# One more batch turned by VectorE, one list of requests for SyncE, and a new order at head and drain

## The chip, the cores and the metric

The kernel runs on one core of a Trainium2 chip, and the metric is the device time of that one core in microseconds. TensorE (PE) multiplies, VectorE (DVE), ScalarE (ACT) and GpSimd (POOL) do the elementwise work, and SyncE (SP) issues most of the DMA requests; ACT issues the others. The requests of SP go through DMA queue q1, those of ACT through q10, and both are served by the same 16 DMA engines.

## The reference

Two inputs `x` ("rgb") and `ctx` ("geo") of 16 batches, each 128 channels by 1024 positions in f32, attend to each other across channels, with 8 heads of 16 channels:

```python
rgb = jnp.transpose(rgb_emb, (0, 2, 1)); geo = jnp.transpose(geo_emb, (0, 2, 1))
def heads(x, w):
    return (x @ w.T).reshape(b, n, H, d).transpose(0, 2, 1, 3)
def xca(q, k, v):
    attn = softmax(einsum('bhni,bhnj->bhij', q, k) * scale, axis=-1)
    return einsum('bhnd,bhde->bhne', v, attn).transpose(0, 2, 1, 3).reshape(b, n, c)
res_p2r = xca(heads(rgb, wq_rgb), heads(geo, wk_point), heads(geo, wv_point)) @ proj_p2r.T
res_r2p = xca(heads(geo, wq_point), heads(rgb, wk_rgb), heads(rgb, wv_rgb)) @ proj_r2p.T
return transpose(rgb + res_p2r) + transpose(geo + res_r2p)
```

## The kernel before

Since the attention is over channels, everything that depends on positions enters through one 128x128 Gram matrix of a batch, `gt` times `xt`. For it both inputs must lie with the positions on the partitions ("turned"). A batch then goes through these products: turn (`turn_half`, only for some batches), Gram matrix (`gram_half`, two halves), `uv_product`, `s_product` (the scores), masking, exponents and `normalise` (the two softmaxes), `y_product`, `t_product` (a 256-column matrix, to which the identity is added for the residual), and the last product (`last_product`, two halves), which multiplies that matrix with `x` and `ctx` and yields the output. The last product is made of twelve 512-column matmuls, since each f32 operand is split in a high and a low fp32r part: ACT makes the high parts (`split_hi`, `t_high`), POOL the low parts of the inputs and DVE the other low parts.

The program is a pipeline written out by hand. In step i (the loop `for i in range(...)` that each engine has) batch i is turned, i-1 goes through the Gram matrix, i-2 through `uv` and `s`, i-3 through softmax, `y` and `t`, and i-4 through the last product. A step of PE begins with the last product of batch i-4. Each engine runs its list in the order written and waits at semaphores.

There are two ways of turning. Batches in `on_tensor` (0 to 4 and 9) are turned by PE with an identity matrix: eight groups of four matmuls into `xt_ps` and `gt_ps`, copied out by ACT (`copy_xt`) and DVE (`copy_gt`). Batches in `VECTOR_GROUPS`, five pairs, are loaded a second time with their 32x32 blocks already exchanged by the DMA (`load_turned`, into one of three slots of `xz` and `gz`) and DVE turns each block (L534). Such a pair is eight requests of 256 KB, four of SP and four of ACT. Groups 0, 1 and 2 are requested in steps 2, 4 and 6 (`first_steps`), groups 3 and 4 in the step after the last batch of the group whose slot they take has been turned.

Besides, every batch is loaded plainly (`load_plain`, two requests of 512 KB into one of six slots), and every output is stored by SP (`store`, 512 KB, from one of eight slots of `out_sb`). ACT's `evacuate(b, 0)` for b from 8 on waits until the store of batch b-8 has landed (L434). SP runs its requests step by step, L236 to L252; the stores come with a lag of seven steps.

Of the kernel before, what the change touches and what calls it, by code (L numbers as in the profile page):

```python
# [15 lines left out]
RAW_SLOTS = 6  # L16
SPLIT_SLOTS = 3
OUT_SLOTS = 8
STORE_LAG = 7
PAIRS = 3  # L20
OFF_HEAD = -3.0e38
WARM = 36
# [1 line left out]
WQR, WKR, WKP, WQP, PP, PR, WVP, WVR = range(8)  # L24


VECTOR_GROUPS = ((5, 6), (7, 8), (10, 11), (12, 13), (14, 15))


def bass_cross_channel_attention(nc: bass.Bass, x, ctx, weights, out):  # L30
# [20 lines left out]
    with ExitStack() as stack:  # L51
# [120 lines left out]
                eng.wait_ge(xt_copied, 2 * on_tensor.index(b) + 1 + half)  # L172


        first_steps = (2, 4, 6)
        issued_in = {first_steps[group] if group < PAIRS else VECTOR_GROUPS[group - PAIRS][-1] + 1: group
                     for group in range(len(VECTOR_GROUPS))}

# [35 lines left out]
        def _(sp):  # L214
            def load_plain(b):
                slot = b % RAW_SLOTS
                sp.dma_start(x_raw[:, slot, :], x[b]).then_inc(x_loaded[slot], 16)
                sp.dma_start(g_raw[:, slot, :], ctx[b]).then_inc(g_loaded[slot], 16)

            def store(b):  # L220
                sp.wait_ge(half_copied, 2 * b + 2)
                sp.dma_start(out[b], out_sb[:, b % OUT_SLOTS, :]).then_inc(out_stored[b % OUT_SLOTS], 16)
# [9 lines left out]

            for i in range(2, B):  # L236
                for b in range(5, B):
                    if i == max(2, b - 1 if b in on_vector else b - 3):
                        if b >= RAW_SLOTS:
                            sp.wait_ge(x_lo_ready, b - RAW_SLOTS + 1)  # L240
                            sp.wait_ge(g_lo_ready, b - RAW_SLOTS + 1)
                        load_plain(b)
                group = issued_in.get(i)
                if group is not None:
                    if group >= PAIRS:
                        pair_turned(sp, group - PAIRS)
                    load_turned(sp, x_turn, xz, xz_loaded, group, (0, 1))
                    load_turned(sp, g_turn, gz, gz_loaded, group, (0, 1))
                if i >= STORE_LAG:
                    store(i - STORE_LAG)  # L250
            for b in range(B - STORE_LAG, B - 1):
                store(b)  # L252
            last_slot = (B - 1) % OUT_SLOTS
            sp.wait_ge(half_copied, 2 * B - 1)
# [11 lines left out]
        def _(pe):  # L266
# [8 lines left out]
                                               ident2[:, 0, :])  # L275
                last.then_inc(done, 1)

            def turn_half(b, half):
                n = on_tensor.index(b)
                if n or half:  # L280

                    pe.wait_ge(xt_copied, 2 * n + half)
                turn(b, half, x_raw, x_first, x_loaded, xt_ps, xt_done)
                if n or half:
                    pe.wait_ge(gt_ready, 2 * b + 1 if half else 2 * on_tensor[n - 1] + 2)
                turn(b, half, g_raw, g_first, g_loaded, gt_ps, gt_done)

            def gram_half(b, half):
                x_turned_half(pe, b, half)
# [80 lines left out]
                nc.tensor.matmul(ps[:, P:2 * P], w_sb[:, WQP, :], uv[:, 1, :], start=True,  # L370
                                 stop=True).then_inc(s_done, 1)

            for i in range(B + 1):
                g, s, y, l = i - 1, i - 2, i - 3, i - 4
                if l >= 0:
                    last_product(l, 0)
                    if l != B - 4:
                        last_product(l, 1)
                    uv_product(s)
                if i in on_tensor:  # L380
                    turn_half(i, 0)
                if s >= 0 and l < 0:
                    uv_product(s)
                if y >= 0 and i not in on_tensor:
                    y_product(y)
                if g >= 0:
                    gram_half(g, 0)
                if y >= 0 and i in on_tensor:
                    y_product(y)
                if i in on_tensor:  # L390
                    turn_half(i, 1)
                if y >= 0:
                    t_product(y)
                if g >= 0:
                    gram_half(g, 1)
                if s >= 0:
                    s_product(s, s_ps)
# [8 lines left out]
            last_product(B - 3, 0, 3, 6)  # L406
            t_product(B - 2)
            last_product(B - 3, 1)
            y_product(B - 1)
            last_product(B - 2, 0, 0, 3)  # L410
            t_product(B - 1)
            last_product(B - 2, 0, 3, 6)
            last_product(B - 2, 1)
            last_product(B - 1, 0)
            pe.wait_ge(half_copied, 2 * B - 2)
# [5 lines left out]
        def _(act):  # L421
# [49 lines left out]
            for i in range(B + 1):  # L471
# [13 lines left out]
                    evacuate(l, 0)  # L485
                if l >= 0 and l != B - 4:
                    evacuate(l, 1)
                if group is not None:
                    load_turned(act, g_turn, gz, gz_loaded, group, (2,))
                if s >= 0:  # L490
                    copy_uv(s)
                if i in on_tensor:
                    copy_xt(i, 0)
                if group is not None:
                    load_turned(act, g_turn, gz, gz_loaded, group, (3,))
                if s >= 0:
                    split_hi(s, g_raw, g_loaded, g_hi, g_hi_ready)
                if i in on_tensor:
                    copy_xt(i, 1)
                if y >= 0:  # L500
                    t_high(y)
                if i == 1:
                    act.wait_ge(wu_loaded, 16)
                    nc.scalar.copy(wu_hi[:, :, :], w_sb[:, WQR:WKR + 1, :]).then_inc(wu_hi_ready, 1)
# [3 lines left out]
            copy_uv(B - 1)  # L508
            evacuate(B - 4, 1)
            split_hi(B - 1, x_raw, x_loaded, x_hi, x_hi_ready)  # L510
            evacuate(B - 3, 0)
            exponents(B - 1)
            t_high(B - 2)
            split_hi(B - 1, g_raw, g_loaded, g_hi, g_hi_ready)
            evacuate(B - 3, 1)
            evacuate(B - 2, 0)
            t_high(B - 1)
            evacuate(B - 2, 1)
# [136 lines left out]
```

## Time and profile before

| | |
|---|---|
| median of 3 runs | 127.03 us (125.57 to 127.28) |
| the profiled execution | 126.98 us, its span 124.9 us, 2.08 us lie around the span |
| PE busy | 117.1 us, 94% of the span |
| DVE, ACT, POOL busy | 59%, 67%, 62% |
| DMA | 36.35 MB, mean 291 GB/s; q1 73.9% and q10 17.7% of 16 engines' span |
| PE's granted clock | full in all 40 slices |

All times are microseconds from the start of the span. In the chain of waits a row gives the start, the length and what ran. In a timeline the engine, line, operation and shapes follow the start and the length; in brackets stands the idle time of the engine before the instruction and what ended it. "SPq" and "ACTq" are the DMA requests as the issuing sequencer runs them. "DMA to landing" is the time from the start of a request to the arrival of its last byte. PE's steps can be found in the chain by their last product (`out_ps L316 x12`).

### The profile page before, as it was taken

The numbers are of one execution on the slowest core, as the hardware profiler recorded it, in microseconds if no ns is written. First come the engines' busy times: TensorE is split into PE (matmuls) and PEld (weight loads), VectorE is DVE, ScalarE is ACT, GpSimd is POOL, SyncE is SP. The second block draws the span as 40 slices with busy tenths as digits, with TensorE's granted clock in tenths as the row PEclk, the third lists the DMA queues.
The fourth block names the chain that finished last, engine by engine and source line by source line (L and its number), as shares of the span: only waits on it lengthen the run. The fifth ranks groups of instructions, "written<-read, shape, count | busy, mean of one in ns | idle before, by whom it ended". The sixth has DMA issues, their size and how long they took to land.

```text
span 124.9 us, 2597 instructions
## 1 busy us (share of the span) xinstructions
PE 117.1 (94%) x826; PEld 106.1 (85%) x826; DVE 73.4 (59%) x214; ACT 84.2 (67%) x191; POOL 77.7 (62%) x41
## 2 busy tenths in 40 slices
PE   6869999999999999699999999999999999997991
PEld 6749898899898989598998989898989897985880
DVE  0035344725969595686259695959696965545210
ACT  4132869694878773886948777776877778588351
POOL 5000597877295955787772959593979595937700
PEclk9999999999999999999999999999999999999999
DMA  3999999999999999999999999999999997003435
GB/s 102 359 407 414 412 311 298 310 302 252 293 277 308 275 329 253 263 317 285 245 240 387 372 269 217 307 306 413 418 420 420 417 417 306 37 30 140 165 144 199
DMA packets 18669, 36.35 MB, mean 291 GB/s; under 512 B 1504, under 2 KB 12128, under 8 KB 18656
## 3 DMA queue, kind: packets, MB, share of 16 engines
q1 hardware_dynamic: 12928, 30.41, 73.9%
q10 hardware_dynamic: 5728, 5.77, 17.7%
q8 instruction: 7, 0.11, 0.4%
q14 instruction: 6, 0.05, 0.1%
HBM read 27.79 MB, written 8.39 MB: 290 GB/s over the span
## 4 chain that ended last, share of the span: by engine, by line
PE 79%; DMA 6%; issue 5%; ACT 4%; DVE 1%; ACTq 1%; SPq 1%
PE out_ps L316 33%; PE gram_bank L295 20%; DMA g_raw<-in_ctx_dram 6%; PE sy_bank L346 5%; PE gt_ps L274 3%; PE xt_ps L274 3%; PE t_bank L359 3%; PE sy_bank L370 3%; PE t_bank L360 3%; PE sy_bank L369 3%; ACT probs L456 2%; ACTq L158 1%; PE uv_bank L339 1%; PE uv_bank L337 1%; PE uv_bank L338 1%
## 5 line engine op out<-in xcount | busy, mean ns | idle before, releaser
L207 POOL TENSOR_TENSOR x_lo<-x_raw,x_hi 128x1024 fp32r<-128x1024 f32 x16 | 38.0, 2378 | 34.8 <-ACT x_hi L429 34.8
L210 POOL TENSOR_TENSOR g_lo<-g_raw,g_hi 128x1024 fp32r<-128x1024 f32 x16 | 38.1, 2382 | 4.3 <-ACT g_hi L429 4.2
L295 PE MATMUL gram_bank<-gt,xt 128*128 128x128 f32 x256 | 33.8, 275 | 0.0
L295 PEld LDWEIGHTS gram_bank<-gt,xt 128*128 128x128 f32 x256 | 31.2, 192 | 0.0
L436 ACT COPY out_sb<-out_ps 128x512 f32<-128x512 f32 x31 | 17.9, 582 | 5.7 <-PE out_ps L316 5.6
L429 ACT CAST g_hi<-g_raw 128x1024 fp32r<-128x1024 f32 x16 | 16.9, 1055 | 2.3 <-issue 2.2
L456 ACT ACTIVATE probs<-probs,min_neg 128x128 f32<-128x128 f32 x32 | 12.6, 395 | 7.8 <-DVE min_neg L553 7.8
L541 DVE COPY gt<-gt_ps 128x512 f32<-128x512 f32 x12 | 8.3, 689 | 15.2 <-PE gt_ps L274 15.2
L429 ACT CAST x_hi<-x_raw 128x1024 fp32r<-128x1024 f32 x16 | 16.6, 1037 | 0.6 <-DMA x_raw<-in_x_dram 0.6
L316 PE MATMUL out_ps<-x_hi,t_hi 128*128 128x512 f32 x31 | 13.6, 440 | 1.0 <-ACT t_hi L469 1.0
L534 DVE STREAM_TRANSPOSE gt<-gz 128x512 f32<-128x512 f32 x20 | 14.0, 702 | 0.0
L534 DVE STREAM_TRANSPOSE xt<-xz 128x512 f32<-128x512 f32 x20 | 13.7, 685 | 0.0
L316 PE MATMUL out_ps<-g_lo,t_hi 128*128 128x512 f32 x31 | 12.4, 401 | 0.0
L442 ACT COPY xt<-xt_ps 128x512 f32<-128x512 f32 x12 | 7.0, 587 | 7.8 <-PE xt_ps L274 7.8
L316 PE MATMUL out_ps<-x_lo,t_hi 128*128 128x512 f32 x31 | 12.3, 397 | 0.0
L469 ACT CAST t_hi<-t_bank 128x256 fp32r<-128x256 f32 x16 | 5.9, 372 | 9.4 <-DVE t_bank L580 9.4
L316 PE MATMUL out_ps<-g_hi,t_lo 128*128 128x512 f32 x31 | 12.3, 395 | 0.0
L316 PE MATMUL out_ps<-g_hi,t_hi 128*128 128x512 f32 x31 | 12.2, 395 | 0.0
L316 PE MATMUL out_ps<-x_hi,t_lo 128*128 128x512 f32 x31 | 12.2, 394 | 0.0
L576 DVE COPY y_sb<-sy_bank 128x256 f32<-128x256 f32 x16 | 6.8, 425 | 8.8 <-PE sy_bank L346 8.8
L580 DVE TENSOR_TENSOR t_bank<-t_bank,ident 128x256 f32<-128x256 f32 x16 | 6.9, 433 | 8.5 <-PE t_bank L360 8.5
L586 DVE TENSOR_TENSOR t_lo<-t_bank,t_hi 128x256 fp32r<-128x256 f32 x16 | 6.8, 422 | 7.4 <-ACT t_hi L469 7.4
(80 smaller groups left out, 205.2 us busy)
## 6 DMA issues: line engine op xcount, KB each, us to landing
x_raw<-in_x_dram SPq DMA_DIRECT2D x15, 512.0 KB, 14.6
g_raw<-in_ctx_dram SPq DMA_DIRECT2D x15, 512.0 KB, 15.2
out_dram<-out_sb SPq DMA_DIRECT2D x15, 512.0 KB, 14.6
xz<-in_x_dram SPq DMA_DIRECT2D x10, 256.0 KB, 13.4
gz<-in_ctx_dram SPq DMA_DIRECT2D x10, 256.0 KB, 14.1
xz<-in_x_dram ACTq DMA_DIRECT2D x10, 256.0 KB, 10.9
gz<-in_ctx_dram ACTq DMA_DIRECT2D x10, 256.0 KB, 14.1
x_raw<-in_x_dram SPq DMA_DIRECT2D x2, 256.0 KB, 4.4
```

Of the source, the lines that this page charges most:

```text
L207: nc.gpsimd.tensor_tensor(x_lo[:, slot, :], x_raw[:, raw_slot, :], x_hi[:, slot, :].bitcast(F32), ALU.subtract).then_inc(x_lo_ready, 1)
L210: nc.gpsimd.tensor_tensor(g_lo[:, slot, :], g_raw[:, raw_slot, :], g_hi[:, slot, :].bitcast(F32), ALU.subtract).then_inc(g_lo_ready, 1)
L274: last = nc.tensor.transpose(ps[:, t * TILE:(t + 1) * TILE], raw[:, b % RAW_SLOTS, cols], ident2[:, 0, :])
L295: last = nc.tensor.matmul(gram_ps, xt[:, b % 2, cols], gt[:, b % 2, cols], start=(t == 0), stop=(t == TILES - 1))
L316: last = nc.tensor.matmul(out_ps[:, cols], w[:, b % 2, which, :], moving[:, slot, cols], start=(n == 0), stop=(n == len(parts) - 1))
L429: nc.scalar.copy(hi[:, b % SPLIT_SLOTS, :], raw[:, b % RAW_SLOTS, :]).then_inc(hi_ready, 1)
L436: nc.scalar.copy(out_sb[:, b % OUT_SLOTS, cols], out_ps[:, cols]).then_inc(half_copied, 1)
L442: nc.scalar.copy(xt[:, b % 2, half * HALF:(half + 1) * HALF], xt_ps[:, :]).then_inc(xt_copied, 1)
L456: nc.scalar.activation(probs[:, a, :], probs[:, a, :], ACT.Exp, bias=min_neg[:, a:a + 1], scale=-1.0, accum_out=row_sum[:, a:a + 1]).then_ ...
L534: nc.vector.transpose(dst[:, b % 2, cols].rearrange("p (j a k) -> p j a k", a=QUADS, k=QUAD), blocks[:, first:first + TILES // 2, :, :]).t ...
L541: nc.vector.tensor_copy(gt[:, b % 2, half * HALF:(half + 1) * HALF], gt_ps[:, :]).then_inc(gt_ready, 1)
L580: nc.vector.tensor_tensor(t_both, t_both, ident2[:, :, :], ALU.add).then_inc(t_summed, 1)
```

## The change

Batch 9 moves from `on_tensor` to DVE: the groups become (5, 6), (7, 8), (9, 10), (11, 12), (13, 14) and (15,), eleven batches instead of ten. Group 2 is requested by ACT in step 5 instead of 6, and there is a sixth group of one batch, which ACT requests in step 11. SP's requests stand in one list: after the first five batches they alternate as written in the diff; stores 0 to 3 come between the loads, and stores 4 to 14 after the last load. ACT's two requests for `gz` move from the middle of a step to its end. At the head PE's `gram_half(0, ...)` comes between the turning of batch 1; in the drain three instructions of PE move and ACT's exponents of batch 15 come ahead of an evacuation.

```diff
-VECTOR_GROUPS = ((5, 6), (7, 8), (10, 11), (12, 13), (14, 15))
+VECTOR_GROUPS = ((5, 6), (7, 8), (9, 10), (11, 12), (13, 14), (15,))
...
-        first_steps = (2, 4, 6)
+        first_steps = (2, 4, 5)
...
+            def load_group(group):
+                if group >= PAIRS:
+                    pair_turned(sp, group - PAIRS)
+                load_turned(sp, x_turn, xz, xz_loaded, group, (0, 1))
+                load_turned(sp, g_turn, gz, gz_loaded, group, (0, 1))
...
-            for i in range(2, B):
-                for b in range(5, B):
-                    if i == max(2, b - 1 if b in on_vector else b - 3):
...
-                if i >= STORE_LAG:
-                    store(i - STORE_LAG)
-            for b in range(B - STORE_LAG, B - 1):
+            load_group(0)
+            load_plain(5)
+            load_group(1)
+            load_plain(6)
+            load_plain(7)
+            load_group(2)
+            load_plain(8)
+            load_plain(9)
+            load_group(3)
+            load_plain(10)
+            store(0)
+            load_plain(11)
+            load_group(4)
+            store(1)
+            load_plain(12)
+            store(2)
+            load_plain(13)
+            load_group(5)
+            store(3)
+            load_plain(14)
+            load_plain(15)
+            for b in range(4, B - 1):
                 store(b)
...
+            turn_half(0, 0)
+            turn_half(0, 1)
+            turn_x(1, 0)
+            gram_half(0, 0)
+            turn_g(1, 0)
+            turn_x(1, 1)
+            gram_half(0, 1)
+            turn_g(1, 1)
+
+            for i in range(2, B + 1):
...
+            last_product(B - 2, 0, 0, 3)
             y_product(B - 1)
-            last_product(B - 2, 0, 0, 3)
+            last_product(B - 2, 0, 3, 6)
             t_product(B - 1)
-            last_product(B - 2, 0, 3, 6)
             last_product(B - 2, 1)
...
-                if group is not None:
-                    load_turned(act, g_turn, gz, gz_loaded, group, (2,))
                 if s >= 0:
                     copy_uv(s)
...
-                if group is not None:
-                    load_turned(act, g_turn, gz, gz_loaded, group, (3,))
...
                 if y >= 0:
                     t_high(y)
+
+                if group is not None:
+                    load_turned(act, g_turn, gz, gz_loaded, group, (2, 3))
...
+            exponents(B - 1)
             evacuate(B - 3, 0)
-            exponents(B - 1)
             t_high(B - 2)
+            evacuate(B - 3, 1)
             split_hi(B - 1, g_raw, g_loaded, g_hi, g_hi_ready)
-            evacuate(B - 3, 1)
             evacuate(B - 2, 0)
```

Three places show how instructions move. The first is SP, around turned group 4. Before, the two stores of batches 0 and 1, the loads of 10, group 4, the store of 2 and the loads of 11 followed each other:

```order
L222 DMA out_dram<-out_sb 128x1024 x2
L217 DMA x_raw<-in_x_dram 128x1024
L218 DMA g_raw<-in_ctx_dram 128x1024
L158 DMA xz<-in_x_dram 32x8x256 x2
L158 DMA gz<-in_ctx_dram 32x8x256 x2
L222 DMA out_dram<-out_sb 128x1024
L217 DMA x_raw<-in_x_dram 128x1024
L218 DMA g_raw<-in_ctx_dram 128x1024
```

Now, from the store of batch 0, the loads of 11, group 4, the store of 1, the loads of 12 and the store of 2:

```order
L230 DMA out_dram<-out_sb 128x1024
L219 DMA x_raw<-in_x_dram 128x1024
L220 DMA g_raw<-in_ctx_dram 128x1024
L157 DMA xz<-in_x_dram 32x8x256 x2
L157 DMA gz<-in_ctx_dram 32x8x256 x2
L230 DMA out_dram<-out_sb 128x1024
L219 DMA x_raw<-in_x_dram 128x1024
L220 DMA g_raw<-in_ctx_dram 128x1024
L230 DMA out_dram<-out_sb 128x1024
```

The loads of batch 11 went ahead of group 4, the store of batch 1 behind it.

The second is ACT in step 7, where group 3 is requested. Before:

```order
L429 CAST x_hi<-x_raw 128x1024
L158 DMA xz<-in_x_dram 32x8x256 x2
L436 COPY out_sb<-out_ps 128x512 x2
L158 DMA gz<-in_ctx_dram 32x8x256
L463 COPY uv<-uv_bank 128x256
L158 DMA gz<-in_ctx_dram 32x8x256
L429 CAST g_hi<-g_raw 128x1024
L469 CAST t_hi<-t_bank 128x256
L451 CAST gram_hi<-gram_bank 128x128
```

Now:

```order
L459 CAST x_hi<-x_raw 128x1024
L157 DMA xz<-in_x_dram 32x8x256 x2
L466 COPY out_sb<-out_ps 128x512 x2
L493 COPY uv<-uv_bank 128x256
L459 CAST g_hi<-g_raw 128x1024
L499 CAST t_hi<-t_bank 128x256
L157 DMA gz<-in_ctx_dram 32x8x256 x2
L481 CAST gram_hi<-gram_bank 128x128
```

Both `gz` requests stand behind `t_hi` and ahead of the next step's `gram_hi`.

The third is PE in the drain, from the end of the last product of batch 13. Before, it was `y` of batch 15, half of a product of batch 14 and `t` of batch 15:

```order
L346 MATMUL sy_bank<-w_sb,probs 128x128 x2
L316 MATMUL out_ps<-x_hi,t_hi 128x512
L316 MATMUL out_ps<-g_hi,t_hi 128x512
L316 MATMUL out_ps<-x_lo,t_hi 128x512
L359 MATMUL t_bank<-w_sb,y_sb 128x128
```

Now:

```order
L336 MATMUL out_ps<-x_hi,t_hi 128x512
L336 MATMUL out_ps<-g_hi,t_hi 128x512
L336 MATMUL out_ps<-x_lo,t_hi 128x512
L366 MATMUL sy_bank<-w_sb,probs 128x128 x2
L336 MATMUL out_ps<-g_lo,t_hi 128x512
L336 MATMUL out_ps<-x_hi,t_lo 128x512
L336 MATMUL out_ps<-g_hi,t_lo 128x512
L379 MATMUL t_bank<-w_sb,y_sb 128x128
```

Three matmuls of batch 14 now stand ahead of `y` of batch 15, and three between `y` and `t`.

## Rows read from the trace of the kernel before

**Rows 1.** The page: DMA busy in tenths, in 40 slices of the span.
```profile
DMA  3999999999999999999999999999999997003435
```

**Rows 2.** Chain of waits, PE's steps 7 to 16 by their last product.
```profile
43.84 2.82 PE out_ps L316 x12
...
57.61 2.81 PE out_ps L316 x12
...
65.64 2.80 PE out_ps L316 x12
...
84.48 2.80 PE out_ps L316 x12
...
90.77 2.80 PE out_ps L316 x12
```

**Rows 3.** Chain of waits, one of batch 9's turnings on PE.
```profile
60.77 0.44 PE xt_ps L274 x4
```

**Rows 4.** Timeline of ACT in step 7.
```profile
46.69 2.92 ACTq L158 DMA_DIRECT2D gz<-in_ctx_dram  x2
...
49.70 1.04 ACT L429 CAST g_hi<-g_raw 128x1024 fp32r<-128x1024 f32 x1 [2.17 <-issue]
```

**Rows 5.** Drain: PE's timeline, then ACT's.
```profile
115.28 0.68 PE L346 MATMUL sy_bank<-w_sb,probs 128*128 128x128 f32 x4 [0.64 <-DVE probs L568]
...
112.83 0.59 ACT L436 COPY out_sb<-out_ps 128x512 f32<-128x512 f32 x1 [0.49 <-PE out_ps L316]
```

**Rows 6.** Head: timeline of DVE, the last turned half of batch 1.
```profile
11.62 0.69 DVE L541 COPY gt<-gt_ps 128x512 f32<-128x512 f32 x1 [1.07 <-PE gt_ps L274]
```

**Rows 7.** Busy time of each engine by stretch; last three: clock, DMA share, GB/s.
```profile
70.00:80.00 10.00, 10.00 (x70) 9.10 (x69) 7.86 (x25) 7.10 (x19) 7.51 (x4) 1.00 1.09 275
90.00:100.00 10.00, 10.00 (x65) 8.92 (x65) 8.27 (x25) 7.72 (x20) 7.65 (x4) 1.00 1.03 419
105.00:115.00 10.00, 9.34 (x62) 8.12 (x61) 4.84 (x19) 7.71 (x20) 7.11 (x3) 1.00 0.21 86
```

**Rows 8.** Requests of SP: load 8, `gz` of group 4, load 11, store 4.
```profile
42.73 0.40 SPq L217 DMA_DIRECT2D x_raw<-in_x_dram  x1
...
L158 SPq DMA_DIRECT2D gz<-in_ctx_dram x2: 1386/2364/3342, 66.9 to 68.4; - x2
...
74.04 0.41 SPq L217 DMA_DIRECT2D x_raw<-in_x_dram  x1
...
76.78 1.86 SPq L222 DMA_DIRECT2D out_dram<-out_sb  x1
```

**Rows 9.** Landing times of the requests of rows 8, in their order.
```profile
DMA to landing us min/median/max: 20.6/20.6/20.6
...
DMA to landing us min/median/max: 12.3/14.0/15.8
...
DMA to landing us min/median/max: 12.3/12.3/12.3
...
DMA to landing us min/median/max: 15.8/15.8/15.8
```

**Rows 10.** Step 13: ACT's evacuations and `t_hi`; DVE's turning and `y_sb`.
```profile
87.31 1.06 ACT L436 COPY out_sb<-out_ps 128x512 f32<-128x512 f32 x2
...
89.93 0.37 ACT L469 CAST t_hi<-t_bank 128x256 fp32r<-128x256 f32 x1 [0.34 <-DVE t_bank L580]
...
86.31 0.70 DVE L534 STREAM_TRANSPOSE gt<-gz 128x512 f32<-128x512 f32 x1
...
88.12 0.42 DVE L576 COPY y_sb<-sy_bank 128x256 f32<-128x256 f32 x1 [0.51 <-PE sy_bank L346]
```

**Rows 11.** ACT in step 16, and the `t_hi` that follows.
```profile
105.42 0.57 ACT L436 COPY out_sb<-out_ps 128x512 f32<-128x512 f32 x1
...
107.91 0.37 ACT L469 CAST t_hi<-t_bank 128x256 fp32r<-128x256 f32 x1 [0.70 <-DVE t_bank L580]
```

More of the change, by code:

```diff
@@ L18 @@
 OUT_SLOTS = 8
-STORE_LAG = 7
 PAIRS = 3
@@ L216, in load_plain @@
                 slot = b % RAW_SLOTS
+                if b >= RAW_SLOTS:
+                    sp.wait_ge(x_lo_ready, b - RAW_SLOTS + 1)
+                    sp.wait_ge(g_lo_ready, b - RAW_SLOTS + 1)
                 sp.dma_start(x_raw[:, slot, :], x[b]).then_inc(x_loaded[slot], 16)
                 sp.dma_start(g_raw[:, slot, :], ctx[b]).then_inc(g_loaded[slot], 16)
+            def load_group(group):
[3 more added lines that the diff above has]
+                load_turned(sp, g_turn, gz, gz_loaded, group, (0, 1))
             def store(b):
@@ L231, in _ @@
             load_plain(4)
-            for i in range(2, B):
-                for b in range(5, B):
-                    if i == max(2, b - 1 if b in on_vector else b - 3):
[L239 to L243, printed above, removed]
-                if group is not None:
[L245 to L248, printed above, removed]
-                if i >= STORE_LAG:
-                    store(i - STORE_LAG)
-            for b in range(B - STORE_LAG, B - 1):
+            load_group(0)
[20 more added lines that the diff above has]
+            for b in range(4, B - 1):
                 store(b)
@@ L276, in turn, with turn_x @@
                 last.then_inc(done, 1)
-            def turn_half(b, half):
+            def turn_x(b, half):
                 n = on_tensor.index(b)
@@ L283, in turn_half, with turn_g @@
                 turn(b, half, x_raw, x_first, x_loaded, xt_ps, xt_done)
+            def turn_g(b, half):
+                n = on_tensor.index(b)
                 if n or half:
@@ L286, in turn_half @@
                 turn(b, half, g_raw, g_first, g_loaded, gt_ps, gt_done)
+            def turn_half(b, half):
+                turn_x(b, half)
+                turn_g(b, half)
             def gram_half(b, half):
@@ L371, in s_product @@
                                  stop=True).then_inc(s_done, 1)
-            for i in range(B + 1):
+            turn_half(0, 0)
[7 more added lines that the diff above has]
+            for i in range(2, B + 1):
                 g, s, y, l = i - 1, i - 2, i - 3, i - 4
@@ L493, in _ @@
                     copy_xt(i, 0)
-                if group is not None:
-                    load_turned(act, g_turn, gz, gz_loaded, group, (3,))
                 if s >= 0:
```

## The prediction

> **What bounds the kernel now.** The page comes first: PE is busy for 117.1 of 124.9 us, so whatever PE does not execute or does not wait for is gained, as long as nothing else is late. But the DMA line is at 9 tenths or more from the second slice to the 34th, to about 106 us [rows 1], so there are two bounds beside each other. The second view is the chain of waits. The last products mark PE's steps: between steps in which no batch is turned by PE it is 6.28 us (84.48 to 90.77), while step 9, where PE turns batch 9, takes 65.64 - 57.61 = 8.03 us [rows 2]. From step 7 to step 9 there are 13.77 us instead of twice 6.28, so 1.21 us were lost; ACT's timeline shows where: two `gz` requests kept it for 2.92 us, `g_hi` waited 2.17 us, and `t_hi` behind it released PE late [rows 4]. The third view is the busy time by stretch. Where the turned loads run, the DMA engines are fully taken at only 275 GB/s; with plain transfers alone they move 419 GB/s [rows 7]. After 105 us they are mostly idle. The fourth view is the landing of single requests. They take 12 to 21 us [rows 8, 9], which is queueing: I read them as a line of work that the engines serve without a break.
>
> **What PE and ACT save.** PE no longer turns batch 9: four groups of 0.44 us [rows 3], 1.75 us, which is what step 9 has over the others (8.03 - 6.28). DVE pays four transpositions of 0.7 us in place of two copies of the same length, 1.4 us more in a step in which it has room (it waited 0.51 us even behind the turning, [rows 10]): nothing. ACT loses two copies: nothing, as it doesn't set the pace.
>
> ACT's `gz` requests go behind `t_hi`. The lost 1.21 us of step 7 goes if the queue has room. Before, groups 2 and 3 were requested in steps 6 and 7; now in 5 and 7. Taken: 1.21 us gained. Between the ends nothing (the requests stall at the new place as long, and there hold up `gram_high` and the exponents) and 1.21, I take the upper, since the four requests of group 2 have one step more to drain.
>
> The head: PE puts a half of batch 0's Gram matrix where it waited for `ctx` of batch 1. But the `uv` product waits for DVE, which copies the last turned half of batch 1 at 11.62 [rows 6] before it can make the low parts. That half is now turned behind another Gram half and comes 0 to 0.2 us later. I take 0; ends -0.2 and +0.7, the latter being a full Gram half less.
>
> The drain: PE waits 0.64 us for the normalised probabilities of batch 15, since ACT evacuates first and takes the exponents later [rows 5]. With three matmuls ahead and the exponents one evacuation (0.59 us) earlier, that wait goes: 0.65 us gained. Its lower end is 0.2, as `g_hi` of batch 15 falls behind an evacuation of 0.59 us and POOL's `g_lo` gets just in time.
>
> So far 1.75 + 1.21 + 0.65 = 3.6 us, and PE's steps 9 to 14 would start at 56.4, 62.7, 69.0, 75.2, 81.5 and 87.8.
>
> **What the DMA engines must do for it.** A plain transfer is 0.524 MB, at 419 GB/s 1.25 us [rows 7]. A turned batch costs more. Load 8 landed at 42.73 + 20.6 = 63.3 and load 11 at 74.04 + 12.3 = 86.3 [rows 8, 9]; in these 23.0 us the engines moved seven plain transfers (8.7 us) and some 2.9 MB of turned data, that is 4.8 us for a turned batch (1.05 MB). The sixth group adds these 4.8 us, half of them through ACT's queue, and everything is wanted 3 us earlier.
>
> Group 4 must be there for DVE in step 13 now, not 14. Its last `gz` request landed at 68.4 + 15.8 = 84.2 [rows 8, 9]. In the new list, at the end of group 4, stores 1 and 2 (before the landing of load 11 at 86.3) are not yet served, `ctx` of 11 is: 86.3 - 1.25 = 85.1. ACT requests group 5 in step 11, at about 70 and 75 us, in the other queue; its half, 2.4 us, is served beside. I take 1.9 of the 2.4: 87.0. Ends 85.1 (nothing overtakes) and 87.5. That the queues are served side by side I read from the DMA share: 1.09 where both have work, 1.03 where only SP's has [rows 7]. The Trainium skill ("DMA: Bandwidth & Descriptors", section "Queues, rings and completion order") says that each DMA engine takes packets in turns from the queues that have work. By that rule all 2.4 us would be in front, group 4 at 87.5 and the time 0.5 us above my sum. No row here follows single packets.
>
> DVE wants `gz` 1.83 us into the step (86.31 - 84.48, [rows 2, 10]), at 83.3: it waits about 3.7 us, and `y`, `t` and `t_high` hang on it. Store 1 comes behind group 4 and lands at 87.0 + 1.25 = 88.2 (86.3 to 88.7). `evacuate(9, 0)` needs that store, for the slot in `out_sb`. Before, it had landed long ago; now ACT, which comes there at about 83.6, waits 4.6 us. From the evacuation to `t_hi` ACT needs 89.93 - 0.34 - 87.31 = 2.28 us [rows 10], and from there 0.4 us to PE's step: step 14 starts at 88.25 + 2.7 = 90.95. By DVE's side it is the same: `gz` at 87.0, two transpositions to `y_sb` at 88.4, and from there 2.4 us of `t`, Gram half and `s` to 90.8. Step 14 began at 90.77 before. So the 3.0 us saved until there are spent: 0.15 us later than before. Smaller lateness ahead of it (group 3 in step 11, store 0 in step 12, about 1 us each, mostly in DVE's and ACT's slack) doesn't count, as step 13 waits for an absolute time.
>
> Behind it the next dates hold: at 104.8 us store 4 lands (before 76.78 + 15.8 = 92.6, [rows 8, 9]; ahead of it are now six plain transfers more, 7.4 us, and group 5, 4.8 us), and ACT's `evacuate(12, 0)` in step 16, at 105.42 before [rows 11], needs it.
>
> **The sum.** Step 14 +0.15, drain -0.65, head 0: the span is 124.9 - 0.5 = 124.4. With the 2.08 us around it 126.5 us against the profiled 126.98, which is 0.05 below the median of 127.03. I forecast 126.5 us, no change that can be told: about 2% (2.5 us) is what a measurement of this kernel can tell.
>
> **The rivals.**
>
> 1. Partly supplied, chance 0.22. Step 13 waits less, because the second half of group 5 doesn't overtake or turned data moves faster side by side in two queues; then store 4 decides. ACT can be there 0.5 us earlier than before, and `t_hi` had 0.70 us of idle time [rows 11]: at most 1.2 us, with the drain 1.85: 125.1 us. For it: if a turned batch takes 4.4 us, it is even 124.7. Against it: two things at once, group 4 and store 1, must be early.
>
> 2. The supply is not the bound, chance 0.17. The landing times of before are those of requests issued as early as the queue took them, not as needed; the new list puts loads by need. Then all of 3.6 us shows: 123.4 us. For it: only one wait of ACT on a load (0.6 us) is seen before. Against it: rows 1 and 7, and that the moved stores have dates too. On the same side a rule of the Trainium skill speaks the other way: "DMA: Bandwidth & Descriptors", section "Specifications", puts the HBM limit of a core at about 358 GB/s, by which a plain transfer would cost 1.46 us; the 419 GB/s of rows 7 contradict it, so it is left out of the sum.
>
> 3. Slower, chance 0.12: store 1 and group 4 later than counted. The place is again step 13: `evacuate(9, 0)`. Each microsecond by which store 1 lands later delays step 14 by one. It is slower by 2% if store 1 lands at 91.3 or later, 3 us behind my sum; at 91.5 the time is 129.8 us. The price would come from the four queued parts of groups 4 and 5 slowing each other: SP's `gz` requests took up to 3.3 us to be issued already [rows 8]. Against it: the sum starts from a measured landing at 86.3, with little between.
>
> 4. The turning by DVE of batch 9 saves PE nothing, because DVE comes late in steps 9 and 11 for its own data. That is in the forecast, since step 13 covers it: its time is the same 126.5 us.
>
> **How the numbers follow.** Forecast with rival 4: 0.49; rivals 0.22, 0.17 and 0.12. The forecast's own range is 125.2 to 127.4: from store 4 as the bound to store 1 at 88.7 with a drain that yields 0.2. The range to hold 8 in 10 reaches down past rival 1 to 124.3 and up to 128.3, where a lateness of 2 us more lies; rival 2 and the far end of rival 3 are left out. Faster by over 2% (below 124.5): rival 2 and a bit of rival 1, 0.20. Slower by over 2%: rival 3 in part, 0.11. Within: 0.69.
>
> **What would show it.** Right: no `L274` in step 9 and a step pitch of 6.28 us to step 11 or 12; step 7 without ACT's 2.17 us; then in step 13 an idle time of DVE before a transposition, ended by `gz`, and of ACT before `out_sb`, ended by the DMA to `out_dram`, of 3 to 5 us; step 14 at 90 to 92; DMA at 9 tenths to about slice 37; PE's 0.64 us in the drain gone. Wrong: step 14 near 88 (rival 2), or a wait for a store in step 16 as the only one (rival 1), or a stall behind ACT's requests at the end of step 5 or 7, which would matter only if step 13 does not wait.

## The result and the profile after

The changed kernel took 133.76 us as the median of four runs, against 126.46 us before: slower, ratio 1.0485 (95% interval 1.0315 to 1.0655). The profiled execution is one of 131.91 us with a span of 129.9 us. So it is 5.0 us more of span, where I had 0.5 us less. The ratios below leave disturbed executions out; where too few were left, no ratio is given.

The page of the changed kernel first, with its lines for PE, PE's clock and the DMA engines:

```profile
PE   6888999999999999999999339999999998999970
...
PEclk9999999999999999999999965899999999999999
DMA  3999999999999999999999999999999999823352
```

PE, nearly full before, has a hole of two slices at 72 to 78 us, and around it its granted clock falls for the only time. The DMA line is full for one slice more than in [rows 1], and these slices are longer. The second view is the chain of waits, and in it the stretch around the hole:

```profile
53.18 22.85 DMA gz<-in_ctx_dram
...
77.73 0.80 PE t_bank L379 x2
78.53 0.43 PE t_bank L380 x2
78.95 1.71 PE gram_bank L315 x8
80.66 0.43 PE sy_bank L389 x2
81.08 0.44 PE sy_bank L390 x2
```

The chain goes back to a request made at 53.18: the last `gz` part of group 3, which lands at 76.03, 22.85 us later. The PE timeline gives the starts of the steps (first 512-column matmul of each), first steps 11 and 14 of the kernel before, then steps 8 to 14 of the changed one:

```profile
71.68 0.48 PE L316 MATMUL out_ps<-x_hi,t_hi 128*128 128x512 f32 x1
...
90.52 0.48 PE L316 MATMUL out_ps<-x_hi,t_hi 128*128 128x512 f32 x1
```

```profile
49.80 0.48 PE L336 MATMUL out_ps<-x_hi,t_hi 128*128 128x512 f32 x1
...
56.08 0.48 PE L336 MATMUL out_ps<-x_hi,t_hi 128*128 128x512 f32 x1
...
62.36 0.48 PE L336 MATMUL out_ps<-x_hi,t_hi 128*128 128x512 f32 x1
...
68.64 0.48 PE L336 MATMUL out_ps<-x_hi,t_hi 128*128 128x512 f32 x1
...
81.16 0.77 PE L336 MATMUL out_ps<-x_hi,t_hi 128*128 128x512 f32 x1
...
87.95 0.48 PE L336 MATMUL out_ps<-x_hi,t_hi 128*128 128x512 f32 x1
...
94.49 0.50 PE L336 MATMUL out_ps<-x_hi,t_hi 128*128 128x512 f32 x1
```

Steps 8, 9 and 10 take 6.28 us each; step 11 starts at 68.64, 3.0 us earlier than before. Then step 11 takes 12.52 us, step 12 takes 6.79, step 13 takes 6.54, and step 14 begins at 94.49 instead of 90.52, 4.0 us later. (In the chain of [rows 2] the same steps of the kernel before begin 0.25 us later than in this timeline, so starts are compared within one view only.) Who waited, by the timelines of DVE and ACT in steps 11 and 13:

```profile
72.29 0.71 DVE L563 STREAM_TRANSPOSE xt<-xz 128x512 f32<-128x512 f32 x1 [2.66 <-DMA xz<-in_x_dram]
76.06 0.71 DVE L563 STREAM_TRANSPOSE gt<-gz 128x512 f32<-128x512 f32 x1 [2.21 <-DMA gz<-in_ctx_dram]
...
90.89 0.71 DVE L563 STREAM_TRANSPOSE gt<-gz 128x512 f32<-128x512 f32 x1 [0.78 <-DMA gz<-in_ctx_dram]
...
91.87 1.08 ACT L466 COPY out_sb<-out_ps 128x512 f32<-128x512 f32 x2 [1.48 <-DMA out_dram<-out_sb]
```

Without waits the `gz` transposition of step 11 would start some 2.07 us into the step (before, in step 13, 86.31 [rows 10] against a start of 84.24 in the PE timeline), at 70.7; it starts at 76.06, 5.3 us later. Last the clock, by stretch:

```profile
74.00:76.00 2.00, 1.64 (x12) 1.39 (x12) 0.00 (x0) 0.00 (x0) 2.00 (x1) 0.85 1.06 354
76.00:78.00 2.00, 0.27 (x1) 0.27 (x2) 1.94 (x4) 0.00 (x0) 0.26 (x1) 0.50 1.05 319
78.00:80.00 2.00, 2.00 (x10) 2.00 (x11) 0.86 (x3) 0.37 (x1) 0.00 (x0) 0.50 1.10 236
80.00:82.00 2.00, 2.00 (x10) 1.90 (x9) 0.73 (x6) 0.38 (x2) 0.00 (x0) 0.50 1.12 219
```

PE idled twice for about 2 us, 1.97 ahead of `y` (at 74.00) and 2.09 ahead of `t` (at 77.73). In the short work between the two, at about 75.4, the granted clock fell to 0.50, the lower level (1.2 GHz), and it stayed there until about 82.2. The eight Gram passes that take 0.89 us at 2.4 GHz took 1.71 us. From `t` to the next step there are 81.16 - 77.73 = 3.43 us, which in step 10, without a wait, are 68.64 - 66.93 = 1.71 us: 1.7 us of step 11's loss come from the clock, and step 12 takes another 0.5 us more than 6.28, as its first matmuls still run slowly (0.77 us where 0.48 is usual).

The rest: from step 14 to the first matmul after step 16 the difference grows from 4.0 to 4.4 us, PE's drain is 0.6 us shorter, and the last store, requested at 126.44, lands after 3.0 us instead of 1.9. That is not the queue of the 11 stores at the end of the list: ten of them had landed by 122.44. The last of them, of batch 14, requested at 123.62, took 4.6 us (2.6 before); why is not shown.

### The profile page after: what moved, and what is told of

It is laid out like the page before. It is cut to its first block, busy times and chain, and to the rows that moved or that the text cites. A ratio compares the mean times of both kernels' runs of the same rounds, so it can differ in the third digit from the quotient of the medians.

```text
span 129.9 us, 2571 instructions
## 1 busy us (share of the span) xinstructions
PE 118.6 (91%) x810; PEld 106.5 (82%) x810; DVE 75.4 (58%) x216; ACT 82.5 (64%) x189; POOL 77.9 (60%) x41
## 3 DMA queue, kind: packets, MB, share of 16 engines
q10 hardware_dynamic: 6304, 6.29, 18.6%
## 4 chain that ended last, share of the span: by engine, by line
DMA 36%; PE 34%; SPq 11%; ACT 6%; DVE 5%; issue 4%; POOL 2%; ACTq 0%; DVEq 0%; POOLq 0%
DMA gz<-in_ctx_dram 18%; DMA out_dram<-out_sb 13%; PE out_ps L336 11%; PE gram_bank L315 8%; SPq L157 6%; DMA x_raw<-in_x_dram 5%; SPq L220 3%; PE gt_ps L287 3%; PE xt_ps L287 3%; PE sy_bank L366 2%; ACT probs L486 2%; POOL x_lo L206 2%; PE t_bank L379 2%; SPq L219 2%; DVE xt L563 1%
## 5 line engine op out<-in xcount | busy, mean ns | idle before, releaser
L315 PE MATMUL gram_bank<-gt,xt 128*128 128x128 f32 x256 | 34.7, 280 | 0.0
L315 PEld LDWEIGHTS gram_bank<-gt,xt 128*128 128x128 f32 x256 | 32.0, 196 | 0.0
L563 DVE STREAM_TRANSPOSE gt<-gz 128x512 f32<-128x512 f32 x22 | 15.4, 702 | 3.5 <-DMA gz<-in_ctx_dram 3.5
L563 DVE STREAM_TRANSPOSE xt<-xz 128x512 f32<-128x512 f32 x22 | 15.1, 686 | 3.2 <-DMA xz<-in_x_dram 3.2
L459 ACT CAST x_hi<-x_raw 128x1024 fp32r<-128x1024 f32 x16 | 16.6, 1035 | 0.0
L570 DVE COPY gt<-gt_ps 128x512 f32<-128x512 f32 x10 | 6.9, 688 | 12.9 <-PE gt_ps L287 12.9
L366 PE MATMUL sy_bank<-w_sb,probs 128*128 128x128 f32 x64 | 10.0, 279 | 2.5 <-DVE probs L597 2.5
L366 PEld LDWEIGHTS sy_bank<-w_sb,probs 128*128 128x128 f32 x64 | 8.4, 190 | 3.6 <-issue 3.6
```

The source lines that it names most:

```text
L315: last = nc.tensor.matmul(gram_ps, xt[:, b % 2, cols], gt[:, b % 2, cols], start=(t == 0), stop=(t == TILES - 1))
L366: last = nc.tensor.matmul(y_ps[:, a * P:(a + 1) * P], probs[:, a, :], w_sb[:, wv, :], start=True, stop=True)
L459: nc.scalar.copy(hi[:, b % SPLIT_SLOTS, :], raw[:, b % RAW_SLOTS, :]).then_inc(hi_ready, 1)
L563: nc.vector.transpose(dst[:, b % 2, cols].rearrange("p (j a k) -> p j a k", a=QUADS, k=QUAD), blocks[:, first:first + TILES // 2, :, :]).t ...
L570: nc.vector.tensor_copy(gt[:, b % 2, half * HALF:(half + 1) * HALF], gt_ps[:, :]).then_inc(gt_ready, 1)
```

## The experiments

Four kernels take the change apart, each against the kernel before. **Groups only:**

```diff
-VECTOR_GROUPS = ((5, 6), (7, 8), (10, 11), (12, 13), (14, 15))
+VECTOR_GROUPS = ((5, 6), (7, 8), (9, 10), (11, 12), (13, 14), (15,))
```

> The kernel before with the eleven-batch groups and nothing else changed. Theory 1 (the eleventh turned batch overloads the DMA engines, whatever the order of requests): the waits of VectorE on xz or gz and of ScalarE on a store stay, 129 to 132 us. Theory 2 (the single list is to blame: batch 9's plain load stands ahead of group 3, stores stand behind loads): group 3 lands 2.5 us or more earlier, step 11 has no long wait, 124 to 127 us.

131.57 us, ratio 1.0324 (1.0186 to 1.0462). This is what the first theory forecast. Nothing waits for group 3, which lands at 68.8; step 11 takes 7.35 us, as ACT waits 2.29 us there for the plain load of batch 9. The longest wait is ACT's for the plain load of batch 11 in step 13:

```profile
89.68 1.04 ACT L429 CAST x_hi<-x_raw 128x1024 fp32r<-128x1024 f32 x1 [5.30 <-DMA x_raw<-in_x_dram]
```

The eleventh batch makes the kernel slow by itself; the list only decides which transfer is late.

**Order only.** The change's head, drain and place of ACT's `gz` requests, with the groups and SP's list of before. Against the change:

```diff
-VECTOR_GROUPS = ((5, 6), (7, 8), (9, 10), (11, 12), (13, 14), (15,))
+VECTOR_GROUPS = ((5, 6), (7, 8), (10, 11), (12, 13), (14, 15))
...
-        first_steps = (2, 4, 5)
+        first_steps = (2, 4, 6)
...
-            load_group(0)
-            load_plain(5)
...
+            for i in range(2, B):
+                for b in range(5, B):
+                    if i == max(2, b - 1 if b in on_vector else b - 3):
+                        load_plain(b)
```

> The change without its groups and without the single list: only the head, the drain and ScalarE's gz requests at the end of a step. Theory 1 and 2 both: the 1.2 us of step 7 and the 0.64 us wait of the drain go, with 0.4 us at the head: 124.0 to 125.0 us. Rival: the requests stall at their new place and hold up gram_hi, so that nothing is gained: 126 to 127 us.

124.61 to 129.88 us in four executions, no ratio. In its trace (126.71 us) the gains on PE are there (step 11 begins at 69.96 instead of 71.68), but in step 13 ACT waits 3.27 us for the load of batch 11. Neither expectation holds for it: ACT's requests hold up nothing, but what PE gains the loads take back. Only the shortest execution lies in the range of the first.

**Without group 3:**

```diff
+                if group == 3:
+                    return
...
+                group = None if group == 3 else group
```

> The change with the turned loads of group 3 left out (2.1 MB; VectorE turns what its slot still holds, so batches 11 and 12 are computed from other data). If the DMA engines are what step 11 and 13 wait for: no wait of VectorE on xz or gz, none of ScalarE on a store, steps of 6.28 us throughout, PE's clock at its upper level all the time, 122.5 to 124.5 us. If something else makes the change slow (VectorE's own time, the order of instructions): 129 us or more.

This kernel leaves 2.1 MB of loads out, so batches 11 and 12 are computed from old data; the instructions are the same. 124.81 us, ratio 0.9856 (0.9768 to 0.9945). The waits on a DMA in all of the kernel:

```profile
DVE gt L566 <- DMA gz<-in_ctx_dram: 2.9, 2, 1.7
...
PE xt_ps L289 <- DMA x_raw<-in_x_dram: 0.2, 1, 0.2
```

With 2.1 MB less to move PE's clock stays at 1.0, and steps 10 to 15 take 6.28 or 6.29 us each. The profiled execution (124.95 us) is 7.0 us shorter than that of the change. DVE, ACT and PE can do the eleven batches; the transfers cannot. The short waits of DVE that remain (1.75 and 1.15 us for `gz`) are for groups 1 and 2, ahead of the missing one; steps 7 and 9 take 7.37 and 6.78 us by them.

**Filled wait.** Twenty warming matmuls ahead of `y` of step 11, and twenty ahead of `t`:

```diff
+                if i == 11:
+                    pe.wait_ge(xt_copied, 2 * len(on_tensor))
+                    for _ in range(20):
+                        nc.tensor.matmul(xt_ps[:, 0:P], warm[:, :], warm[:, :], start=True, stop=True)
                 if y >= 0 and i not in on_tensor:
                     y_product(y)
...
+                if i == 11:
+                    for _ in range(20):
+                        nc.tensor.matmul(xt_ps[:, 0:P], warm[:, :], warm[:, :], start=True, stop=True)
                 if y >= 0:
                     t_product(y)
```

> The change with twenty small bf16 matmuls without use ahead of y and twenty ahead of t in step 11, where PE waits about 2 us each. If the fall of PE's granted clock to 0.77 and 0.89 comes from these waits and costs 1.5 to 2 us by slow matmuls behind them: the clock stays at 1.0, and step 11 takes 10.5 to 11.0 us instead of 12.5. The total stays within 1 us of the change's, since store 1 is the next date. If the clock falls for another reason, step 11 stays at 12.5 us or longer.

133.17 us in its one execution, and inconclusive: here the wait for group 3 was longer (4.08 us on `xz`), PE still idled 3.37 us, and step 11 took 13.8 us. The clock fell, but later and for a shorter time:

```profile
76.00:78.00 2.00, 0.38 (x3) 0.41 (x4) 1.47 (x1) 0.00 (x0) 1.19 (x1) 1.00 1.04 337
78.00:80.00 2.00, 2.00 (x15) 1.94 (x14) 1.75 (x4) 0.00 (x0) 0.00 (x0) 0.60 1.08 219
80.00:82.00 2.00, 2.00 (x21) 2.00 (x19) 0.48 (x1) 0.00 (x0) 0.00 (x0) 0.55 1.12 210
82.00:84.00 2.00, 2.00 (x18) 1.96 (x18) 1.04 (x3) 0.37 (x1) 0.00 (x0) 1.00 0.91 169
```

That the waits bring the clock down fits: ahead of the drain it falls only in the six traces in which a step takes over 10 us (10.49 to 15.13), and not in the second trace of the change, whose longest step is one of 9.81. What filling the waits would give is not shown.

**Transfers alone.** A kernel that only loads and stores, stretch after stretch: (1) turned loads by both queues, SP quarters 0 and 1, ACT 2 and 3; (2) turned, SP alone; (3) plain by SP beside turned by ACT; (4) plain alone; (5) single-batch turned groups; (6) four stores beside turned loads by ACT; (7) as 1, SP quarters 0 and 2, ACT 1 and 3. Its core:

```diff
+            for q in quads:
+                into = z[q * QUAD:(q + 1) * QUAD, slot, 0:count, :]
+                eng.dma_start(into.rearrange("p e (a m) -> p (e a) m", a=4),
+                              src[q][:, 4 * first:4 * (first + count), :]).then_inc(done, 16)
+        def phase_end(eng, n):
+            eng.wait_ge(sp_sems[n], 16 * sp_count[n])
```

> No computation, only transfers (the output is zeros), in stretches that end before the next begins: turned loads by both queues (4.2 MB), turned loads by SyncE alone (4.2 MB), plain loads by SyncE beside turned loads by ScalarE (4.2 and 2.1 MB), plain loads alone (4.2 MB), single-batch turned loads by both (2.1 MB), stores beside turned loads, and turned loads with the partition quarters crossed. If costs add (a turned batch of 1.05 MB 4.8 us wherever it stands, a plain transfer 1.25 us): 19, 19, 20, 10, 10, 15, 19 us. If turned loads in both queues at once slow each other: stretches 1 and 2 at more than 21 us, and stretch 3 below 19 us, since plain packets fill gaps. If a group of one batch is dearer: stretch 5 over 11 us.

The stretches took 16.2, 21.8, 24.9, 13.0, 10.3, 15.9 and 19.6 us, start and landing included. By added prices they were to take 19, 19, 20, 10, 10, 15 and 19: turned loads in both queues are cheaper, and turned loads beside plain ones, stretch 3, far dearer. Single-batch groups are not dearer. From the DMA view of stretches within 1, 2 and 3 (4 to 14, 20 to 35 and 44 to 50 us; packets, bytes, mean rate, and for the last the queues' packets, MB and shares):

```profile
DMA packets 3199, 3.09 MB, mean 309 GB/s; under 512 B 179, under 2 KB 3199, under 8 KB 3199
...
DMA packets 3429, 3.31 MB, mean 220 GB/s; under 512 B 202, under 2 KB 3429, under 8 KB 3429
...
DMA packets 830, 1.91 MB, mean 318 GB/s; under 512 B 64, under 2 KB 464, under 8 KB 830
q1 hardware_dynamic: 412, 1.50, 80.6%
q10 hardware_dynamic: 418, 0.41, 23.1%
```

Busy shares above 1 and yet 220 or 309 GB/s: a turned batch of 1.05 MB takes 3.4 us when both queues carry such loads, 4.8 us in SP's queue alone, and at the 202 GB/s that ACT's queue reached alone at the end of stretch 3 (59.6 to 61.6 us), 5.2 us. Beside plain loads it is more: of the 6 us from 44 to 50 the 1.50 MB of plain loads are worth 3.6 at 419 GB/s, and the other 2.4 went for 0.41 MB, which is 6.2 us for a turned batch (an estimate from these rows). Costs don't add, and my single price was the one of SP's queue alone. Beside plain loads the queues move packet for packet (412 to 418), whatever the packets' size. By the Trainium skill ("DMA: Bandwidth & Descriptors", section "Queues, rings and completion order") each engine takes packets in turns from the queues that have work; the trace agrees with its 412 and 418.

Four more kernels reorder the requests. All have the new head, drain and places of ACT's requests. **Load 11 first** (ten batches, SP's order as before up to load 10; then, written as an edit of the old order, as below, and stores 3 to 6 stand one load later):

```diff
             load_plain(10)
+            load_plain(11)
             load_group(4)
             store(2)
-            load_plain(11)
```

> Ten turned batches as before, the new head, drain and places of ScalarE's gz requests, SyncE's requests in the order of the kernel before but with the loads of batch 11 ahead of group 4. If the order-only kernel was held up by the date of batch 11 alone (ScalarE waited 3.3 us for it), that wait goes and the time is 123.5 to 125 us in every run. If the engines' total work is the bound, another load is late in its place and the time is 126 us or more.

124.86 to 128.27 us, ratio 0.989 (0.9864 to 0.9916). The ratio rests on two of the four executions only, and the trace is of the longest (128.27 us), so whether this list is better is open. In the trace three plain loads of `x`, of batches 8, 10 and 12, are each about 2 us late for ACT (6.0 us in three waits), and the last load lands at 107.5. The wait moved, it did not go.

**Ten batches, list of the change:**

```diff
+            load_plain(9)
             load_group(2)
             load_plain(8)
-            load_plain(9)
             load_group(3)
...
-            load_group(5)
```

> The same with the list of the change, fitted to ten batches (9 ahead of group 2, group 5 left out): store 0 behind load 10, store 1 behind group 4, stores 4 to 14 behind the last load. If the list is harmless, 123.5 to 125 us and no wait of ScalarE on a store. If the late stores are what the list costs: waits on stores 0 and 1, 126 us or more.

124.95 to 135.69 us, no ratio. Its trace (131.25 us) has the wait that the forecast put at `evacuate(9, 0)`:

```profile
91.31 1.07 ACT L465 COPY out_sb<-out_ps 128x512 f32<-128x512 f32 x2 [5.55 <-DMA out_dram<-out_sb]
```

Here with ten batches: in this execution the late place of store 1 is enough for it. Its shortest execution, 124.95 us, is as short as that of load 11 first (124.86), so the late place need not cost anything.

**Nine batches:**

```diff
+VECTOR_GROUPS = ((5, 6), (7, 8), (10, 11), (12, 13), (15,))
```

> Nine turned batches: batch 14 goes back to PE, otherwise as the kernel with load 11 ahead. PE has 1.75 us more to do, the DMA engines one turned batch (about 5 us) less. If supply binds at ten batches: 125 to 126 us, no wait on a DMA, and less spread than with ten. If supply does not bind at ten: 1.75 us slower than the kernel with load 11 ahead.

134.47 us, and a miss of mine: PE turns batch 14 in step 14 and so needs its plain load two steps earlier, but I left it where it was. PE waits for it: `ctx` of 14 lands at 98.1, and step 14, from 90.36, is 14.45 us long. It says nothing on whether nine would be better.

**Eleven by date:**

```diff
             load_plain(8)
-            load_plain(9)
             load_group(3)
-            load_plain(10)
+            load_plain(9)
             store(0)
+            load_plain(10)
+            store(1)
             load_plain(11)
             load_group(4)
-            store(1)
```

> The change with group 3 ahead of the loads of 9, store 0 ahead of the loads of 10, and store 1 and the loads of 11 ahead of group 4. If the change's list was badly ordered: group 3 lands 3 to 5 us earlier, step 11 has no long wait, 126 us or less. If eleven batches are too much in any order: the lateness moves to group 4 or to a load, 129 to 133 us.

133.74 us, ratio 1.0461 (1.0382 to 1.0541). Group 3 lands 4.8 us earlier than in the change and step 11 takes 7.74 us, but the lateness moves to group 4, as the second theory had it, and step 13 takes 15.13 us:

```profile
91.36 0.71 DVE L563 STREAM_TRANSPOSE xt<-xz 128x512 f32<-128x512 f32 x1 [7.05 <-DMA xz<-in_x_dram]
```

So eleven batches were too much in all three orders tried: the change's, groups only, and this.

**Drain only**, from the kernel before:

```diff
-            y_product(B - 1)
             last_product(B - 2, 0, 0, 3)
-            t_product(B - 1)
+            y_product(B - 1)
             last_product(B - 2, 0, 3, 6)
+            t_product(B - 1)
...
-            evacuate(B - 3, 0)
             exponents(B - 1)
+            evacuate(B - 3, 0)
             t_high(B - 2)
-            split_hi(B - 1, g_raw, g_loaded, g_hi, g_hi_ready)
             evacuate(B - 3, 1)
+            split_hi(B - 1, g_raw, g_loaded, g_hi, g_hi_ready)
```

> The kernel before with the new order in the drain alone. The drain begins when all loads have landed, so what it saves cannot be lost to the DMA engines: PE's wait of 0.64 us goes, 0.4 to 0.65 us less, 0.3 to 0.5% faster. If g_lo of batch 15 then comes late, as ScalarE's cast of it falls behind an evacuation: no change or up to 0.5 us slower.

125.24 us, ratio 0.9895 (0.9813 to 0.9977): about 1% faster than the kernel before, and the only part of the change that is faster by its interval. The chain in the drain:

```profile
112.36 2.09 PE out_ps L316 x9
114.46 0.68 PE sy_bank L346 x4
115.13 0.70 PE out_ps L316 x3
115.83 0.31 PE t_bank L359 x2
116.14 0.22 PE t_bank L360 x2
116.36 2.80 PE out_ps L316 x12
```

PE goes from the last matmul of batch 14's first three into `y` with no wait; in [rows 5] it waited 0.64 us. From the first matmul after step 16 to the last of all PE takes 10.8 us instead of 11.5, so 0.7 of the 1.3 us that the ratio stands for are seen in the drain; the rest is not explained by it.

**Both kernels again**, unchanged, for the spread:

> The kernel before, unchanged, for a second trace of the landing times. If the DMA engines' pace is the same in every execution, the last load (ctx of 15) lands at 102.6 us within 0.5 us again; if the pace varies from run to run, it lands some us off, without a change of the time, as long as no load is late.

> The change, unchanged, for a second trace. If lateness of group 3 in step 11 belongs to the change: VectorE waits again for xz and gz there, 3 to 8 us together, and for store 1 or group 4 in step 13; the last load lands at 109 to 111 us. If the first trace was an accident: steps 11 and 13 under 8 us each.

The kernel before: 126.11 us, the last load at 101.6 instead of 102.5, outside the 0.5 us that I had allowed. The change: 129.79 us, span 127.8, PE's clock 1.0 throughout, the last load at 106.5 instead of 109.4. Neither of my two cases for it holds as a whole: the wait for group 3 is shorter than 3 us, but step 13 takes 9.81. Rates between 20 and 70 us (last number of each row): before, again before, the change, again the change, then order only and load 11 first:

```profile
20.00:70.00 50.00, 48.81 (x344) 44.71 (x343) 33.03 (x96) 36.87 (x84) 34.91 (x15) 1.00 1.08 292
20.00:70.00 50.00, 49.77 (x352) 45.60 (x351) 33.57 (x97) 37.23 (x84) 35.81 (x16) 1.00 1.08 303
20.00:70.00 50.00, 50.00 (x347) 45.78 (x348) 35.63 (x105) 36.74 (x87) 37.19 (x16) 1.00 1.09 279
20.00:70.00 50.00, 48.54 (x340) 44.53 (x340) 34.78 (x100) 35.82 (x83) 36.11 (x16) 1.00 1.08 279
20.00:70.00 50.00, 50.00 (x358) 46.21 (x357) 33.62 (x98) 37.18 (x85) 36.09 (x16) 1.00 1.08 294
20.00:70.00 50.00, 50.00 (x354) 46.05 (x355) 33.29 (x97) 35.52 (x82) 33.70 (x15) 1.00 1.08 279
```

The change is below both of before. But the last two kernels make the same requests in the same order up to load 10 (requested at 61.8 and 64.8), and their paces are 294 and 279 GB/s. So the pace differs by 5% between traces without any difference in the requests, and that the change lowers it is not shown by 279 against 292 and 303.

In the second trace of the change, group 3 costs 1.66 us of waiting, and step 13 goes almost as forecast:

```profile
86.85 0.71 DVE L563 STREAM_TRANSPOSE xt<-xz 128x512 f32<-128x512 f32 x1 [2.10 <-DMA xz<-in_x_dram]
90.09 0.71 DVE L563 STREAM_TRANSPOSE gt<-gz 128x512 f32<-128x512 f32 x1 [1.12 <-DMA gz<-in_ctx_dram]
...
90.90 1.07 ACT L466 COPY out_sb<-out_ps 128x512 f32<-128x512 f32 x2 [4.71 <-DMA out_dram<-out_sb]
```

ACT's wait for store 1 is 4.71 us (forecast: 4.6), but it ends at 90.8 instead of 88.2, and step 14 begins at 93.56, 3.0 us later than in the kernel before.

## Why the prediction was wrong

**What PE saves: right for the turning and the drain, not shown for step 7.** Step 9 takes 6.28 us in both traces of the change, no turning in it. The 1.21 us of step 7 were those of one execution: in the second trace of the kernel before ACT waited there 1.21 us behind its requests, but step 7 took 6.52 us, 0.24 more than 6.28. In the first trace of the change the loss is gone (step 8 at 49.80), in the second step 7 takes 7.84 us, as DVE waits 2.20 us for `gz` of group 1. ACT's requests did stall at a new place, the end of step 4 (2.00 us; `gram_hi` waited 1.74), and step 5 took 6.62 us, 0.3 more. The head gave 0.4 us, where I had put 0 (0.3 by the second traces); that ACT's copy of `xt` no longer stands behind a `gz` request there is my reading of it. The drain gave 0.6 us as forecast, and alone it is the one part of the change that pays, since no load is wanted behind it.

**Supply as the bound, the waits at step 13: right in kind.** DVE waits for group 4, ACT in `evacuate(9, 0)` for store 1. Groups only is slower by 3% with the old list, and the run without group 3 shows that the transfers are the cause.

**The step that failed** is the one that makes dates: landing times of a single trace of the kernel before, taken as fixed, with one price of 4.8 us for a turned batch added. Both halves failed.

The dates first. Ahead of group 3 the two kernels have the same requests, in nearly the same order. Its last part landed at 71.8 in the trace that the sum starts from, and at 76.0 and 74.0 in those of the change, 4.2 and 2.1 us later. Group 4 landed at 90.9 and 90.1 instead of 87.0, store 1 at 91.8 and 90.8 instead of 88.2: most of their lateness was there at group 3. In the other kernels with ten batches and these requests ahead, group 3 landed at 69.2 (drain only), 68.9 (before again), 73.3 (order only), 76.7 (load 11 first) and 76.2 (list of the change), so a sum to a tenth of a microsecond could not stand on one of these landings. Where the slower pace of the change comes from stays open. It is not from fewer stretches with turned loads in both queues: counted by half microseconds with mostly 1 KB packets in both, they fill 24.5 and 26.0 us of 20 to 70 in the traces of the kernel before, and 26.5 and 26.0 in those of the change. Nor do ACT's later requests alone bring it: order only has them too and moves 294 GB/s.

Then the price. By the prediction's own figures (23.0 - 8.7 us for 2.9 MB) a turned batch is 5.2 us, not 4.8; the 312 GB/s that the profile shows in that stretch are 7.2 MB in all, by which it is 4.3. The transfers alone show 3.4 to 6.2 us by what the other queue carries. Over the long stretch this did less harm: from group 4 to the last load the sum has 16.6 us (87.0 to 103.6, which is 102.5 + 4.8 less three stores of 1.25), and it took 18.6 and 16.4. The last load landed at 109.4 and 106.5.

**The term that I waved away:** "group 3 in step 11, about 1 us, mostly in slack, doesn't count, as step 13 waits for an absolute time". DVE wanted group 3 at 70.7 and got it 5.3 us late in the first trace, 1.7 in the second. This lateness was not absorbed, as group 4 and store 1 behind it were late by nearly as much: the date of step 13 is not absolute.

**What was not in the sum at all:** PE's clock. In the first trace, around two waits of 2 us, slow matmuls cost another 1.7 us in step 11 and 0.5 in step 12. The second trace, at 1.0 throughout, was 2.1 us shorter; how much of that is the clock is open.

**Rival 3 came true** and had the right place: `evacuate(9, 0)` and group 4 in step 13. By its rule the times were to be 130.1 us with store 1 at 91.8 and 129.1 with store 1 at 90.8; they were 131.91 and 129.79, and the difference of the first is about what the clock cost. Its reason, parts of groups 4 and 5 slowing each other, is not what made most of the lateness, as group 3 was late already. I gave it 0.12, as the sum seemed to hang on one measured landing with little between. But the forecast had all margins used up on one side: any loss of pace came through one to one, while a better pace was capped by store 4. And the pace was known from one trace, while the last load of the kernel before lands 1 us apart in two, and that of ten batches with ACT's later requests at 103.5, 103.7 and 107.5.

## What to carry to other kernels

When the DMA engines are full up to the last load, work taken off the matmul engine gains nothing if it has to be paid with another load of the same data in small pieces; check first that every transfer still lands in time, and look for gains where no load follows, as in the drain. A price per byte read from one mix of transfers doesn't hold for another, and the landing times of one execution don't hold for the next, so a sum that stands on them needs a range that is wider on the late side, where PE pays for late data with the wait and can pay again with a lower clock behind it.

## What the runs showed of the hardware

- Turned loads (32 partitions, 1 KB pieces): 309 GB/s with both queues at work, 220 with SP's alone, 202 with ACT's alone, 251 with both when the quarters were crossed; plain loads up to 420. All with busy shares of the DMA engines of 1.03 to 1.13 while loads were queued, so the share doesn't tell how much more could be moved.
- Beside each other, 4 KB and 1 KB packets go one for one: 412 to 418 in 6 us.
- Two kernels with the same requests in the same order up to load 10 moved 294 and 279 GB/s from 20 to 70 us. The four executions of the ten-batch kernel with the change's list took 124.95 to 135.69 us, those without group 3 123.73 to 125.61.
- Around two idle times of PE of about 2 us, its granted clock was 0.50 from 75.4 to 82.2 us. Behind a single one of 3.37 us, 0.60 and 0.55 were the means of the two stretches of 2 us from 78 to 82.
